# Two attentions on one core: transposes of the probabilities moved to the head of a unit, and a quarter of one subtraction moved to GpSimd

## The reference

```python
x = x + L0_xattn(layernorm(x), ctx, ctx)      # 16 heads of 8, keys and values from ctx
x = x + L0_ffn(layernorm(x))                  # shared expert + top 2 of 7 experts
x = x + L1_xattn(layernorm(x), ctx, bias...)  # attention to ctx, attention to x, then an LSTM and an FFN
x = x + L1_ffn(layernorm(x))                  # top 1 of 8 experts, with a capacity
```

```python
q = (x @ wq + bq) * 8 ** -0.5;  k = mem @ wk + bk;  v = mem @ wv + bv
w = softmax(q k^T + bias);      o = (w v) @ wo + bo
```

## Time and profile before

| | |
|---|---|
| Time, median of 3 runs | 873.72 us (873.52 to 880.57) |
| The profiled execution, its own time | 878.44 us |
| Its span, first to last instruction | 876.5 us |
| Mean granted TensorE clock | 0.914 of full |
| PE / DVE / ACT / POOL busy in the span | 82% / 51% / 37% / 14% |

### The profile page before, as it was taken

The page is one execution under the profiler, slowest core; times in us unless marked ns, Lnnn a source line. Parts: engine busy times, 40 slices in busy tenths (PEclk is TensorE's granted clock), DMA queues, the critical chain, the costliest instruction groups (busy, mean ns, idle before and its releaser), DMA issues.

```text
span 876.5 us, 16652 instructions
## 1 busy us (share of the span) xinstructions
PE 721.4 (82%) x6370; PEld 593.1 (68%) x6370; DVE 445.0 (51%) x1063; ACT 321.7 (37%) x790; POOL 125.3 (14%) x161
## 2 busy tenths in 40 slices
PE   1788738998999989947878777899999998457993
PEld 1567626887887878836766666699999966343673
DVE  5477655554544545568999999132323220540231
ACT  1376612222222222215666665344444423100331
POOL 3133415000000000001001002000000000006276
PEclk9999956999999999967999999799999969758897
DMA  8210500000000000051111110000000000201322
GB/s 265 69 32 25 162 1 0 1 1 1 0 0 0 0 0 0 27 135 52 38 42 36 36 42 1 1 1 2 1 1 1 1 1 1 48 3 53 62 22 21
DMA packets 29566, 25.97 MB, mean 30 GB/s; under 512 B 3792, under 2 KB 26704, under 8 KB 29136
## 3 DMA queue, kind: packets, MB, share of 16 engines
q1 hardware_dynamic: 26064, 23.23, 9.4%
q0 software_dynamic: 3456, 2.12, 1.8%
HBM read 19.80 MB, written 5.80 MB: 29 GB/s over the span
## 4 chain that ended last, share of the span: by engine, by line
PE 70%; DVE 10%; issue 9%; ACT 6%; POOL 2%; DMA 1%; DVEq 1%; POOLq 0%; ACTq 0%; SPq 0%
PE SC L577 11%; PE PT L587 10%; PE MI L515 6%; PE SC L665 5%; PE PT L506 4%; PE PJ L482 3%; PE PJ L479 2%; PE SC L739 2%; PE SC L498 2%; PE SC L648 2%; PE SC L656 2%; PE SC L704 2%; PE PT L710 2%; PE SC L650 2%; PE SC L649 2%
## 5 line engine op out<-in xcount | busy, mean ns | idle before, releaser
L850 ACT ACTIVATE big<-SC 128x512 f32<-128x512 f32 x88 | 52.6, 598 | 168.4 <-PE SC L577 168.4
L1117 DVE TENSOR_TENSOR big<-SC,big 128x512 f32<-128x512 f32 (+1 forms) x88 | 60.8, 690 | 76.5 <-ACT big L850 76.3
L515 PEld LDWEIGHTS MI<-vblk,PTs 128*64 128x64 f32 x1536 | 51.9, 143 | 61.4 <-issue 42.8
L587 PEld LDWEIGHTS PT<-wd,big 128*128 128x128 f32 (+1 forms) x768 | 90.0, 191 | 2.3
L587 PE MATMUL PT<-wd,big 128*128 128x128 f32 (+1 forms) x768 | 90.2, 274 | 0.0
L515 PE MATMUL MI<-vblk,PTs 128*64 128x18 f32 x1536 | 55.8, 216 | 40.9 <-issue 29.2
L577 PE MATMUL SC<-xP,wgP 128*128 x264 | 80.0, 411 | 10.5 <-DVE X L1112 4.5
L577 PE MATMUL SC<-xP,wuP 128*128 x264 | 74.5, 390 | 0.0
L577 PEld LDWEIGHTS SC<-xP,wgP 128*128 128x128 f32 x264 | 45.4, 188 | 28.6 <-DVE big L1117 9.6
L399 POOL COPY kvs<-xnT 128x256 f32 (+1 forms) x16 | 6.4, 400 | 369.9 <-ACT xnT L776 242.8
L1151 DVE SCALAR_TENSOR_TENSOR lb<-th 128x32 f32<-128x32 f32 x64 | 12.3, 192 | 91.3 <-ACT th L887 91.3
(11 more groups left out here) (194 smaller groups left out, 1369.6 us busy)
## 6 DMA issues: line engine op xcount, KB each, us to landing
kvs<-in_ctxT SPq DMA_DIRECT2D x32, 128.0 KB, 2.1
w1s<-in_e1w SPq DMA_DIRECT2D x8, 256.0 KB, 2.7
w2s<-in_e1w SPq DMA_DIRECT2D x8, 256.0 KB, 3.1
wg<-in_wg SPq DMA_DIRECT2D x1, 1408.0 KB, 8.3
wu<-in_wu SPq DMA_DIRECT2D x1, 1408.0 KB, 11.3
slots_in<-big SPq DMA_DIRECT2D x1, 1300.0 KB, 8.9
big<-slots_in SPq DMA_DIRECT2D x8, 130.0 KB, 2.4
wd<-in_wd SPq DMA_DIRECT2D x2, 512.0 KB, 13.6
```

Of the source, the lines that this page charges most:

```text
L515: last = pe.matmul(MI[S * b:S * b + S, 18 * c:18 * c + 18], PTs[p][:, c, S * b:S * b + S], vblk[v][:, c, b, :, :], start=True, stop=True)
L587: last = pe.matmul(PT[:, e % 2, t * P:t * P + P], h[0:w, t * P:t * P + P], wd[0:w, e, c, :], start=(c == 0), stop=(c == 2))
L850: act.activation(sg[a % 2], SC[:, a % 2, :], ACT.Silu).then_inc(s["silu_done"], 1)
L1117: last = dve.tensor_tensor(hT[e % 2][0:w, c, :], SC[0:w, 2 + a % 2, :], sg[a % 2][0:w, :], ALU.mult)
```

## The change

Four edits. In the first attention the step's list on PE starts with `probs_t(n-1)`, and `scores(n+1)` stands ahead of `out0(n-2)`; the list on ACT starts with `pt_copy(n-1)`, and `v_copy(n+2)` stands behind `xo_copy(n-2)`. In the second attention the lists on PE and ACT start with `probs_t(n-1)` and `pt_copy(n-1)`. The subtraction of the second attention is split by heads: DVE does heads 0 to 11, GpSimd heads 12 to 15 (`upper`), started by the same maximum; `exp` waits for both. On GpSimd, `upper` stands ahead of `kv_copy` and ahead of the copy at L405.

```diff
--- before.py
+++ after.py
@@ -21,6 +21,7 @@
 RG = 4
 HR = H // RG
 NC = H // 2
+HV = 3 * H // 4
 E0, HID = 8, 352
 NR = E0 - 1
 CH = [(0, 128), (128, 128), (256, 96)]
@@ -220,7 +221,7 @@
             prep_done prep_step
             ln_stats ln_newton ln_xn ln_transposed ln_evacuated logits_done logits_copied
             xn_kept x_split w_rounded w_split
-            proj_done q_ready kexp_ready scores_done biased_done max_done soft_done exp_done
+            proj_done q_ready kexp_ready scores_done biased_done max_done soft_done soft_hi_done exp_done
             pt_done pt_copied pv_done recip_done norm_done ot_done ot_copied wo_done xo_ready resid_done
             v_copied fold_done fold_copied l_bias_ready kv_copied g_done g_copied xtm_copied bo_added b2_added x_mid_stored x_mid_loaded
             route_one route_step sig_ready route_done
@@ -399,9 +400,17 @@
                 pool.tensor_copy(kvs[1][:, :, :, :], xnT[:, bass.ds(i * P, P)].rearrange("p (b s) -> p b s", b=2).unsqueeze(2)
                                  .broadcast_to([P, 2, 2, S])).then_inc(s["kv_copied"], 1)
 
+            def upper(i, u):
+                pool.wait_ge(s["max_done"], NU0 + 2 * i + u + 1)
+                hi = sc[u][:, HV:H, :]
+                pool.tensor_tensor(hi, hi, mx[u][:, HV:H].unsqueeze(2).broadcast_to([P, H - HV, S]), ALU.subtract
+                                   ).then_inc(s["soft_hi_done"], 1)
+
             def tile(i, more):
+                upper(i, 0)
                 if more:
                     kv_copy(i + 1)
+                upper(i, 1)
                 pool.tensor_copy(xtm.rearrange("p (t b) -> p b t", b=B)[:, bass.ds(2 * i, 2), :],
                                  xnT[:, bass.ds(i * P, P)].rearrange("p (b t) -> p b t", b=2)).then_inc(s["xtm_copied"], 1)
             kv_copy(0)
@@ -532,16 +541,16 @@
 
             def step0(n, v):
                 p = v % 2
+                if not known(n, 0):
+                    probs_t(n - 1, 1 - p)
                 if not known(n, NU0 - 2, NU0 - 1):
                     proj(0, n + 2, n + 2, p)
                 if not known(n, 0, 1):
                     out_t(n - 2, p)
-                if not known(n, 0):
-                    probs_t(n - 1, 1 - p)
+                if not known(n, NU0 - 1):
+                    scores(n + 1, 1 - p, "soft_done", n + 1)
                 if not known(n, 0, 1):
                     out0(n - 2, p)
-                if not known(n, NU0 - 1):
-                    scores(n + 1, 1 - p, "soft_done", n + 1)
                 if not known(n, 0):
 
                     wait(pe, s["xo_ready"], n - 1)
@@ -611,12 +620,12 @@
             def step1(m, v, i):
 
                 n, p = NU0 + m, v % 2
+                if not known(m, 0):
+                    probs_t(n - 1, 1 - p)
                 if not known(m, NU1 - 2, NU1 - 1):
                     proj(1 + p, n + 2, i + 1, p)
                 if not known(m, 0, 1):
                     out_t(n - 2, p)
-                if not known(m, 0):
-                    probs_t(n - 1, 1 - p)
                 if not known(m, NU1 - 1):
                     scores(n + 1, 1 - p, "biased_done", m + 1)
                 if not known(m, 0):
@@ -789,8 +798,10 @@
                     last = act.activation(vblk[v][64 * h:64 * h + 64, :, :, h, 0:DK], src[:, :, :, h, :], ACT.Copy)
                 last.then_inc(s["v_copied"], 1)
 
-            def exp(n, p):
+            def exp(n, p, second=False):
                 act.wait_ge(s["soft_done"], n + 1)
+                if second:
+                    act.wait_ge(s["soft_hi_done"], n - NU0 + 1)
                 act.activation(sc[p][:, :, :], sc[p][:, :, :], ACT.Exp).then_inc(s["exp_done"], 1)
 
             def pt_copy(n, p):
@@ -821,15 +832,16 @@
 
             def step0(n, v):
                 p = v % 2
+                if not known(n, 0):
+                    pt_copy(n - 1, 1 - p)
                 if not known(n, 0, 1):
                     ot_copy(0, n - 2, p)
                 if not known(n, NU0 - 2, NU0 - 1):
                     q_copy(0, n + 2, p)
-                    v_copy(n + 2, (v + 2) % 4)
-                if not known(n, 0):
-                    pt_copy(n - 1, 1 - p)
                 if not known(n, 0, 1):
                     xo_copy(n - 2, p)
+                if not known(n, NU0 - 2, NU0 - 1):
+                    v_copy(n + 2, (v + 2) % 4)
                 exp(n, p)
             for n in range(2):
                 q_copy(0, n, n)
@@ -857,14 +869,14 @@
 
             def step1(m, v, i):
                 n, p = NU0 + m, v % 2
+                if not known(m, 0):
+                    pt_copy(n - 1, 1 - p)
                 if not known(m, 0, 1):
                     otm_copy(n - 2, p, i - 1)
                 if not known(m, NU1 - 2, NU1 - 1):
                     q_copy(1 + p, n + 2, p)
                     v_copy(n + 2, (v + 2) % 4)
-                if not known(m, 0):
-                    pt_copy(n - 1, 1 - p)
-                exp(n, p)
+                exp(n, p, True)
             for u in range(2):
                 q_copy(1 + u, NU0 + u, u)
                 v_copy(NU0 + u, u)
@@ -1026,7 +1038,8 @@
                     dve.wait_ge(s["biased_done"], n - NU0 + 1)
                     dve.tensor_reduce(mx[p][:, :], t, AX.X, ALU.max).then_inc(s["max_done"], 1)
                     dve.wait_ge(s["max_done"], n + 1)
-                    dve.tensor_tensor(t, t, mx[p][:, :].unsqueeze(2).broadcast_to([P, H, S]), ALU.subtract
+                    lo = t[:, 0:HV, :]
+                    dve.tensor_tensor(lo, lo, mx[p][:, 0:HV].unsqueeze(2).broadcast_to([P, HV, S]), ALU.subtract
                                       ).then_inc(s["soft_done"], 1)
 
             def norm(n, p):
```

## The result

| | before | changed |
|---|---|---|
| Time, median of 4 runs each | 877.14 us | 905.96 us (905.45 to 909.51) |
| Span of the profiled execution | 876.5 us | 907.6 us |
| Mean granted TensorE clock | 0.914 | 0.883 |

The changed kernel takes 1.034 times as long (95% interval 1.031 to 1.038), 28.8 us more by the medians. The forecast was 17.9 us more, 891.6 us, from the 873.72 us that three runs of the kernel before had given. The profiled execution of the changed kernel (909.51 us, clock 0.883) is the slowest of its four; the other three had a clock of 0.894 to 0.895.

The account below looks back on a forecast made before the run. It took a loop through pv, proj, out_t and ACT's copies to bound the first attention, VectorE the second. First attention 11.3, second 4.6 and clock 2 sum to +17.9 us on 873.72: 891.6 us, range 881 to 906.

Parts of the forecast that it names:

- the ring: First attention: loop from v_copy through front, maximum, subtraction, scores, out0 and xo_copy to v_copy, 5.70 us a unit against 4.76.
- The second ring: First attention: loop through exp, transposes, proj, out_t, scores, out0, xo_copy and v_copy, about 5.2 us a unit.
- The term: First attention's whole cost: +10.3 us for eleven slower units and +1 for its start and end, +11.3 us.
- the edges: Start and end of each attention, +1 us each; bounds -1 to +3 given for the first.
- The first leg: Second attention: from v_copy's end to the start of the next unit's exp, 5.23 us.
- The second leg: Second attention: from exp's start to the end of the v_copy behind its transposes, 4.63 us.
- It is the bound: Second attention before the change: VectorE, busy 130.84 of 134.30 us, sets the pace.
- the new ring: Second attention: loop through VectorE and GpSimd, 9.86 us for two units, 4.93 each; +3.6 us over 28 units.
- two falls: TensorE clock dropping to the 1.2 GHz level twice in the attentions, about 1 us each, +2 us; bounds 0 and 20.
- in between: PE's sparse stretches, about 3.1 us (first attention) and 2.9 (second), lie between 2.7 today and 3.15 where the clock fell.
- Rival 1: Both attentions: the TensorE clock falls some 15 times more in sparse stretches, about 906 us; chance 0.15.
- Rivals 2 to 4: Halves run side by side, 881.5 us, chance 0.13; GpSimd goes first, 897 us, 0.06; first attention gains, 872.0 us, 0.05.

Follow-up runs that it names:

- the filling: Two matrix products of constants added on PE ahead of every wait for the exponential, against the changed kernel: 889.66 us, 1.014 times before.

## Why the prediction was right and wrong

**The direction and the places** were right: both attentions, and nothing else of the span.

**First attention, the ring: right.** Computed 5.70 us a unit, measured 5.62 (the usual step); computed 1.9 us of waiting ahead of `front`, measured 2.03. The run with the value copy ahead shows that this copy closes it. The second ring, computed at 5.2, is 5.01. The term was 11.3 us; with the filling it measures 14.2 (86.3 against 72.1). Of these, the second to the thirteenth step at 5.63 for 4.76 are 10.4 us, where I had 10.3 for eleven at 5.70. One of the twelve has a fall (6.58), which adds 1.0. The first step and the last two are 2.8 us longer than before, where I had +1 for the edges.

**Second attention: the mechanism right, its size too big.** The two halves hardly overlap, as read from two rows of before. But GpSimd ended 0.46 us behind VectorE, not 0.59, and two units take 9.57 us (4.79 each), not 9.86 (4.93). With the filling it is +0.1 us in all where I had +4.6. Two units of that kernel at full clock, from the end of one `v_copy` at 506.89 to 516.53, show where the difference lies. The first leg is 5.23 us, just as computed, by luck: GpSimd's 0.13 us less is made up by the bias to the maximum, 1.72 for 1.62, and smaller pieces. The second leg, from the exponential at 512.12 to the end of `v_copy`, is 4.41, not 4.63: the way to the transposes takes 1.11 for 1.17, they take 0.92 for 0.96, and `proj` 0.90 for 1.00. The edges didn't cost the 1 us that I had put there.

**"It is the bound" (VectorE in the second attention): half read.** It was busy 97% of the time, and the split shows that a second ring of the same length stood behind it. The forecast compared the saved 0.25 us with the new ring alone and came out right on that only because the order was changed with it.

**The clock: this is the step that failed.** I took two falls, 2 us. The filling takes away 16.6 us of span-time in the two attentions (5.7 and 10.9), over half of the loss of 31.1. Six steps of each attention are long. The price of 1 us holds in the first; in the second it is about 1.5 us. The rows were the right ones: a sparse stretch of 3.15 us had fallen and 2.7 had held, and the stretch now is as computed, 3.1, in the first attention. What I did wrong was to give "in between" a small number, when a stretch comes back in every unit: six of the first attention's fifteen steps came out 0.8 to 1.1 us above the usual 5.62 (the last, 6.40, is one of the edges). In the second I reckoned with an even 2.9. But a ring over two units is uneven. PE in the changed kernel, second attention:

```profile
558.86 0.69 PE L507 MATMUL SC<-kexp,qT 32*64 32x256 f32 x16
...
561.38 1.06 PE L515 MATMUL PT<-ident,sc 128*128 128x128 f32 x8 [0.67 <-ACT sc L805]
...
563.38 0.69 PE L507 MATMUL SC<-kexp,qT 32*64 32x256 f32 x16
564.02 1.11 PE L524 MATMUL MI<-vblk,PTs 128*64 128x18 f32 x32
566.49 1.94 PE L515 MATMUL PT<-ident,sc 128*128 128x128 f32 x8 [1.35 <-ACT sc L805]
```

From `scores` to the transposes it is 2.52 us in one unit and 3.11 in the next, and behind the second the transposes ran at the 1.2 GHz level. Every step of about 6 us in this attention is of that kind: none came behind a stretch of 2.16 to 2.56 us, and of those of 3.0 to 3.2 us about half. Rival 1 was thus the case: some twelve falls in the steps where I had two, with its cause named and its chance, 0.15, too low. That its 906 us is the measured time is partly luck: the ring of the second attention was 4.5 us cheaper than in its sum, the edges of the first dearer, and the median before 3.4 us higher than the one I started from.

**Rivals 2 to 4** fell: the halves don't run side by side, VectorE went first in all 32 units, by 0.04 to 0.05 us, and the first attention didn't gain.

**The sum.** Forecast 11.3+4.6+2=17.9. In the spans: ring 14.2, split and order of the second attention 0.1, clock 16.6, rest 0.3, together 31.1 up to rounding.

## What to carry to other kernels

In a pipeline of several units, write down the ring from each instruction to itself in the next unit, through every engine's list; a copy moved behind a neighbour in one list can join two rings that were apart, and an engine that is 97% busy can hide a second ring of equal length, so that relieving it gains nothing. Work given to GpSimd that reads SBUF, beside a VectorE instruction with two SBUF inputs, ends behind it: the 0.7 us of a quarter's subtraction came 0.46 us later than VectorE's three quarters. When a change lengthens the time between PE's dense bursts, compare that stretch with one in the same trace after which the clock fell, take the longest of the stretches that alternate, and count how often it comes back. Its length alone doesn't tell whether a given one is followed by a fall.

## What the runs showed of the hardware

- GpSimd's write of zeros ran beside VectorE's two-input subtraction in all 32 units at 0.31 us, while a GpSimd copy, which reads, was held to 0.93 us, 0.25 us behind the subtraction's end. The Trainium skill says so in "SBUF — State Buffer", section "Who interferes with whom" (the contention is with a GpSimd instruction that reads SBUF, not with one that only writes); the trace agrees.
- Equal sparse stretches of PE (3.11 us from `scores` to transposes) were followed by the 2.4 GHz level at 82.87 and by the 1.2 GHz level at 88.59. In the run with the second attention's order alone, two falls came behind 2.77 and 2.84 us, while one stretch of 3.07 (503.86 to 506.93) was followed by transposes at full clock. What decides between them isn't settled by these runs.
- Two products of constants ahead of each group of transposes held the granted clock at 1.00 from 440 to 560 us in the second attention, where PE had stood idle about 0.6 to 1.35 us ahead of each group, without lengthening its steps. In the first attention of the same kernel one fall still came in the middle (transposes of 1.92 us at 64.94). Where there was no gap to fill they cost 0.27 us a unit.
